# GpSimd's row gathers and last scatters, given out by the count of finished expert units

## What is computed

```python
weights = where(adj < 1, exp(-(1/adj - 1)**2 / 0.5), 0)      # every element of adj
x = x + weights @ (layernorm(x) @ W + B)

z = layernorm(x)
logits = z @ gate_w + gate_b                                 # 16 experts
vals, idx = top_k(logits, 2); share = softmax(vals)
moe = sum over the 2 of share * (relu(z @ w1[e] + b1[e]) @ w2[e] + b2[e])
y = z + moe
x = x + layernorm(y) * gamma + beta
```

## Time and profile before

| | |
|---|---|
| runs | 1827.14, 1827.83, 1828.46 us, median 1827.83 |
| profiled execution | span 1823.2 us from first to last instruction; no other time is given of it |
| busy in the span | PE 1624.7 us (89%), DVE 1499.7 (82%), ACT 1565.7 (86%), POOL 463.6 (25%) |
| granted TensorE clock | 0.951 of full speed in the mean |
| DMA | 338.22 MB, 186 GB/s in the mean |
| chain that ended last | PE 84%, DVE 6%, another core or an unknown queue 5%, issue 3% |

### The profile page before, as it was taken

The page is one execution under the profiler, slowest core; times in us unless marked ns, Lnnn a source line. Parts: engine busy times, 40 slices in busy tenths (PEclk is TensorE's granted clock), DMA queues, the critical chain, the costliest instruction groups (busy, mean ns, idle before and its releaser), DMA issues.

```text
span 1823.2 us, 24195 instructions
## 1 busy us (share of the span) xinstructions
PE 1624.7 (89%) x8178; PEld 1073.6 (59%) x8178; DVE 1499.7 (82%) x2298; ACT 1565.7 (86%) x1502; POOL 463.6 (25%) x342
## 2 busy tenths in 40 slices
PE   4999999999999999999999999999999987384720
PEld 3666666666666666666666656666666786373620
DVE  7999998989899999999999989999998443153464
ACT  5899999999999999999999999999999664253531
POOL 0001223131314040407132231313140213535342
PEclk9999999999999999999999999999999999696765
DMA  9559867676767676776776676787673244343431
GB/s 313 158 160 290 235 199 215 195 217 193 214 195 212 196 212 198 220 213 202 210 202 209 199 210 199 209 247 208 202 206 121 80 124 143 87 141 97 129 110 50
DMA packets 216792, 338.22 MB, mean 186 GB/s; under 512 B 18080, under 2 KB 74144, under 8 KB 216544
## 3 DMA queue, kind: packets, MB, share of 16 engines
q1 hardware_dynamic: 208368, 319.62, 59.8%
q0 software_dynamic: 8304, 17.06, 3.1%
HBM read 303.07 MB, written 33.55 MB: 185 GB/s over the span
## 4 chain that ended last, share of the span: by engine, by line
PE 84%; DVE 6%; another core or an unknown queue 5%; issue 3%; ACT 1%; DMA 1%; DVEq 0%; SPq 0%; ACTq 0%
PE acc L1118 48%; PE tp L1137 24%; PE tp L1164 4%; PE tp L1192 3%; PE acc L1192 2%; DVE chunk L654 1%; PE tp L1153 1%; DVE stats L666 1%; DVE chunk L660 1%; DVE chunk L1004 1%; PE misc L1094 1%; ACT chunk L613 1%; DVE msg L729 1%; DMA xs<-in_x_dram 1%
## 5 line engine op out<-in xcount | busy, mean ns | idle before, releaser
L1118 PE MATMUL acc<-wT,msg 128*128 128x512 f32 x2048 | 976.0, 599 | 0.0
L527 ACT ACTIVATE wT<-tp 128x1024 f32<-128x1024 f32 x512 | 761.0, 1674 | 14.0 <-PE tp L1137 12.4
L521 ACT ACTIVATE chunk<-chunk 128x2048 f32<-128x2048 f32 x256 | 655.3, 2560 | 0.1
L660 DVE SCALAR_TENSOR_TENSOR chunk<-chunk 128x2048 f32<-128x2048 f32 x256 | 584.8, 2284 | 54.7 <-ACT chunk L521 54.1
L1137 PEld LDWEIGHTS tp<-ident,chunk 128*128 128x128 f32 x4096 | 478.7, 141 | 223.2 <-issue 221.5
L654 DVE SCALAR_TENSOR_TENSOR chunk<-chunk 128x2048 f32<-128x2048 f32 x256 | 583.5, 2280 | 1.9 <-DMA chunk<-in_adj_dram 1.9
L1137 PE MATMUL tp<-ident,chunk 128*128 128x128 f32 x4096 | 534.3, 274 | 0.0
L516 ACT ACTIVATE chunk<-chunk 128x4096 f32<-128x4096 f32 x118 | 511.0, 4331 | 0.0
L1118 PEld LDWEIGHTS acc<-wT,msg 128*128 128x128 f32 x2048 | 349.1, 190 | 258.3 <-issue 245.8
L457 POOL TENSOR_TENSOR pool_carrier<-pool_carrier 1x1 f32<-1x1 f32 x32 | 43.7, 1365 | 951.5 <-DVE row_now L845 825.9
L476 POOL DMA_INDIRECT rows_in<-y,row_now x128 | 216.7, 1693 | 40.4 <-issue 40.4
(11 more groups left out here) (121 smaller groups left out, 794.7 us busy)
## 6 DMA issues: line engine op xcount, KB each, us to landing
chunk<-in_adj_dram SPq DMA_DIRECT2D x256, 1024.0 KB, 5.4
chunk<-rows_in SPq DMA_DIRECT2D x118, 64.0 KB
rows_out<-chunk SPq DMA_DIRECT2D x59, 128.0 KB
chunk<-rows_in SPq DMA_DIRECT2D x35, 128.0 KB
rows_out<-chunk SPq DMA_DIRECT2D x17, 256.0 KB
y_kept<-y SPq DMA_DIRECT2D x16, 256.0 KB, 6.1
chunk<-y_kept SPq DMA_DIRECT2D x16, 256.0 KB
out_dram<-chunk SPq DMA_DIRECT2D x16, 256.0 KB
```

The source lines that it names most:

```text
L521: act.activation(slot(c), slot(c), ACT.Exp, scale=-1.0).then_inc(inverted, 1)
L527: act.activation(wT[:, (g * PPG + m) % WSLOTS, :], tp[(g * PPG + m) % TSLOTS][:, :], ACT.Exp, scale=-2.0).then_inc(weighted, 1)
L660: dve.scalar_tensor_tensor(out=slot(c), in0=slot(c), scalar=2.0, in1=slot(c), op0=ALU.subtract, op1=ALU.mult).then_inc(squared, 1)
L1118: ins = pe.matmul(acc[:, :], msg[:, n, :], wT[:, (g * PPG + m) % WSLOTS, k * ROWS:(k + 1) * ROWS], start=(n == 0), stop=(n == 2 * PPG - 1))
```

## The change

Two kinds of waits are added on GpSimd, and nothing else. Before each of the last group's eight scatters it waits for `ro_ready` at 52, 53, ... 59. Before each gather of the first two batches it waits for a count, too: for the first batch's gather n (0 to 55) for 73 + n // 2, for the second batch's gather n (0 to 39) for 108 + n. The divisor is the size in tiles of the units that run meanwhile. The third batch's gathers are as before.

```diff
+        SCATTER_AT = 52
+
+        def gather_unit(b, nth):
+
+            return min(UNIT0[b + 1] + 2 + nth // TILES[b + 1], NU)
...
                 for k in range(K):
                     for b in range(TB):
+                        if g == GROUPS - 1:
+                            pool.wait_ge(ro_ready, SCATTER_AT + k * TB + b)
                         pool.indirect_dma_start(
                             rows_in, bass.IndirectOffsetOnAxis(row_now[:, k, b:b + 1].bitcast(U32), 0),
                             y[:, b, :], None).then_inc(scattered, 16)
...
                     carry()
                     for kb in range(KB):
+                        if b + 1 < len(BATCHES):
+                            pool.wait_ge(ro_ready, gather_unit(b, (g - FIRST[b]) * KB + kb))
                         pool.indirect_dma_start(
                             back[g % BACK][:, kb, :], None, rows_out[b],
                             bass.IndirectOffsetOnAxis(row_back[:, g, kb:kb + 1].bitcast(U32), 0)).then_inc(back_in[g % BACK], 16)
```

## The result

The changed kernel takes 1771.54 us (median of 4 runs, 1770.1 to 1772.5) against 1827.72; the ratio is 0.9692, with a 95% interval of 0.9679 to 0.9706. The forecast was 1778.0, the range 1750 to 1816. Its profiled execution has a span of 1769.0 us, 54.2 less than the 1823.2 of before. Of the 6.5 us that the forecast was high, 4.2 lie in the gain (50 forecast) and most of the rest in the step from span to time: 4.6 us were added for the span's distance to the median, which is 2.5 us here.

The account below looks back on a forecast made before the run. Tail bound by TensorE's signals coming late during GpSimd's unbroken gather runs, no engine full. Loss of 97 us cut to 47 saves 50: span 1823.2 to 1773, plus 4.6 to the median, 1778 us; range 1750 to 1816.

Parts of the forecast that it names:

- The bound and the mechanism: Tail: no engine or DMA full; from a GpSimd burst's third gather on, TensorE's signals come late, more so in longer bursts.
- Price of a request today: Tail and last scatters: 96.8 us lost for 104 requests on GpSimd, 0.93 us each.
- about 90: Sign: the changed kernel's second batch in about 90 us (28 units at 2.9, 7 at 2.0).
- about 80: Sign: the changed kernel's third batch in about 80 us.
- Price of a paced request: Waiting gathers and scatters: 0.45 us lost each, 47 us for 104, so 50 us saved.
- The first two gathers do no harm: Bursts in the tail: a burst's first two gathers delay nothing; signals come late from the third on.
- 1.8 us after its end: Burst of eight gathers: TensorE's results are seen again 1.8 us after the end of the last gather.
- the rival of a full drain: Tail and scatters: signals pass only 1.8 us after GpSimd's last request, however short its run; 69 us more, 1897 us; chance 0.11.
- In ones and twos: Sign on the timeline: gathers in ones and twos, with idle times ended by VectorE.
- first group's combination: Its last two gathers are allowed after unit 76, it stands behind unit 79; costed at nothing, else a few us once.
- Full relief: Rival: the stall goes altogether, only 25 us of GpSimd's pace remain, 72 us saved, 1756 us; chance 0.22.
- transfers behind transfers: Rival of nothing changing: the stall is of another making, say transfers behind others; 1828 us; chance 0.07.

Follow-up runs that it names:

- plain transfers: Kernel before, with the first four groups' 32 gathers issued by GpSimd as plain transfers of 128 consecutive rows, no index: 1785.92 us, one run.
- grants of eight: Changed kernel, but a group's eight gathers are all allowed at the count that its first one had: 1789.25 us (0.9804).
- the run with short pauses: Kernel before, no counts, two fills of a scratch tile after each second request, in all batches and the last scatters: 1750.05 us (0.9585).
- fills: Kernel before, with 50 scratch-tile fills on GpSimd, each waited for, right after the last scatters: 1825.36 us, one run.

## Why the prediction was right

**The bound and the mechanism.** Right in the main point: dense indexed requests on GpSimd make the other engines' waits end late, TensorE's signals among them, and the gain is a part of what that costs. The parts add up, other work on GpSimd or plain transfers on its queue don't do it, and a pause without a count brings more than the count. That it is the signal that is late, and not its receiver, the trace of the kernel before shows: its recorded updates of the semaphore that TensorE raises behind a second layer stand at 1535.05, 1546.40 and 1574.44 us, each 0.13 or 0.14 us before VectorE's addition. The requests' own data doesn't pile up: between 1570 and 1575 us, behind the run of 32, 32 packets are left on GpSimd's queue. Why indexed requests do it, I have not found; no run tells what is shared.

**Price of a request today.** I had 96.8 us for 104 requests. Against the free paces of 1.98 and 1.06 us the table gives 124.0 - 35 x 1.98 = 54.7 us for 56 (I had 50.3) and 98.4 - 46 x 1.06 = 49.6 for 40 (I had 38.1), 1.09 each where I had 0.92. My sums took the bursts alone and left out what is slow between them: in the second batch the two units behind the long stall take 5.84 us (additions at 1575.11 and 1580.95) where 3.96 are free, and in the third batch 44.4 us lie outside the bursts, at a lower clock. Apart from that I had cut the batches wrongly. The window from 1529 to 1641.5, called the 35 units of the second batch, holds 410 matmul records, which is 29 units; the batch runs from 1524.5 to 1648.5. So the signs "about 90" and "about 80" us for the changed kernel's batches missed, with 101.2 and 71.9; 28 units at 2.9 us and 7 at 2.0 are 95 us, too, and not 90.

**Price of a paced request.** The term of 0.45 us was the one I chose. Measured by the same free paces it is 0.57 in the second batch (101.2 - 69.3 = 31.9, 56 gathers) and 0.58 in the third (71.9 - 48.8 = 23.1, 40). Both prices were 0.12 to 0.17 us low, so their difference, and the 50 us that I had against 54.2 in the spans, came out near. That is luck in part: 0.45 was picked between bounds, and the two errors happen to go the same way. By stretch: scatters 4.8 forecast, 4.6 measured; second batch 25 and 22.8; third 20 and 26.5.

**"The first two gathers do no harm."** True for a first pair after a long rest, and false as I used it. With 0.59 us of break after each two, stalls come back almost whole. The break, or the wider spacing that comes with it, has to be there as well; 0.97 us was enough for most.

**"1.8 us after its end."** True behind the burst of eight, and not behind the run of 32, where the last request ends at 1569.42 and VectorE's next addition starts 5.15 us later:

```profile
1568.48 0.94 POOL L494 DMA_INDIRECT chunk<-rows_out,row_back  x1 [0.30 <-issue]
...
1574.57 0.42 DVE L989 TENSOR_TENSOR chunk<-acc,blobs 128x256 f32<-128x256 f32 x1 [27.41 <-remote]
```

So what the rival of a full drain took as a fixed time grows with the run.

**"In ones and twos."** Wrong in the second batch: as a pair takes 2.5 us against 1.98, GpSimd ran in sixes and eights, and the count only ended each run; grants of eight did the same. It held roughly in the third batch, and there lies the larger gain. The forecast of a total stall cut, but not gone, was right for both.

**What stays.** After the last unit 76.6 us, forecast 77; first group's combination cost nothing to see; gathers at 985 ns in the mean beside a busier VectorE, not the 1693 of the scatters in the adjacency stage; PEclk 0.92 and 0.95, forecast over 0.8.

**The rivals.** Full relief, 1756 us, didn't come, and the run with short pauses shows that it was there to be had in these stretches (80.4 and 59.7 us). The full drain after each request, the slower case, and no change are out by the time itself; transfers behind transfers as the cause are out by the plain transfers. The rule of the Trainium skill that I weighed there (DMA: Bandwidth & Descriptors, Queues, rings and completion order: the engines take turns between queues after each packet) agrees with the runs, which show 32 plain transfers beside a TensorE that is busy for all of the 17.90 us.

## What to carry to other kernels

Where a helper engine issues many indexed transfers in a row, look at whether the others' waits end only during or after its run, with their releaser long done; if so, space the requests out before moving anything else. A plain pause did more than a tie to the consumers' progress, and it has to be sized: here 0.97 us after two requests worked, 0.59 us after two and 0.97 us after four didn't (requests 1.64, 1.43 and 1.45 us apart). Then count what the pauses cost the helper itself, since the work it feeds will end later: the best total lay where units ran almost free and GpSimd became the last one.

## What the runs showed of the hardware

- Indexed requests of 128 rows each from GpSimd (0.95 us and 0.30 us of idle between) hold up signals of other engines: loss per request from 0.44 us (in eights) to 1.13 us (in 32). Plain ones from the same queue (0.54 us each) didn't, nor did fills.
- In the adjacency stage, where 120 of the scatters run, nothing of the sort is seen: in the 40 slices of the changed kernel's page (busy tenths) PE stays at nine from the second on up to the tail, whatever POOL does. There a scatter takes 1693 ns in the mean, so with its idle time the requests stand some 2.0 us apart (from the earlier trace rows, an estimate), wider than the 1.64 us of the short pauses. Whether that is the reason, no run tells.

```profile
PE   4999999999999999999999999999999999877710
...
POOL 0001131222223131304341313041505021364661
```

- VectorE and ScalarE at the end of the program stood too in the run of 32 (waits of 2 to 4 us between short operations), and the end was 13 us shorter with a break of 0.59 us after two or 0.97 us after four.
- With a break of 0.97 us after two, a request each 1.64 us, most of the loss is gone (about 11 us stay in each batch); with 0.59 us after two, or 0.97 us after four, at 1.43 and 1.45 us a request, nearly nothing is gained in the second batch (117.8 and 114.0 us for 124.0) and about 11 us in the third. I expected a gradual effect. Where between them it turns, whether it hangs on the break or on the spacing, and whether on rows in a request, wasn't tried; nor was a version with pauses during the units only, which by the stretches measured (28.1, 80.4 and 59.7 us, and an end no longer than the changed kernel's 76.6 if its gathers were in time) may be faster than 1750 us.
